# Six transformer layers on one core: the token shift before the feed-forward goes through DMA instead of TensorE, and the transposes of q are evicted bank by bank

## What is computed

```python
def shift_tokens(t):                 # the second half of the channels comes from the token before
    a, s = jnp.split(t, 2, -1)
    s = jnp.pad(s, ((0, 0), (1, 0), (0, 0)))[:, :-1]
    return jnp.concatenate([a, s], -1)
for i in range(6):
    x = attn_layer(shift_tokens(x), Wqkv[i], q_scale[i], k_scale[i], Wo[i]) + x
    x = ffn_layer(shift_tokens(x), ln_g[i], ln_b[i], W1[i], b1[i], W2[i], b2[i]) + x
```

## Time and profile before

| | us |
|---|---|
| median of 3 runs (lowest, highest) | 3981.29 (3973.6, 3982.08) |
| the profiled execution | 3975.59 |
| its span, first to last instruction | 3973.6 |
| TensorE busy | 3731.3 (94%) |
| VectorE busy | 3272.7 (82%) |
| ScalarE busy | 2830.6 (71%) |
| GpSimd busy | 2383.9 (60%) |

### The profile page before, as it was taken

The page is one execution under the profiler, slowest core; times in us unless marked ns, Lnnn a source line. Parts: engine busy times, 40 slices in busy tenths (PEclk is TensorE's granted clock), DMA queues, the critical chain, the costliest instruction groups (busy, mean ns, idle before and its releaser), DMA issues. The chain is left out here.

```text
span 3973.6 us, 160814 instructions
## 1 busy us (share of the span) xinstructions
PE 3731.3 (94%) x70608; PEld 2684.1 (68%) x70608; DVE 3272.7 (82%) x4767; ACT 2830.6 (71%) x4676; POOL 2383.9 (60%) x1968
## 2 busy tenths in 40 slices
PE   5899999967999999999999999999999999999997
PEld 3222222236788878788887888878787888878775
DVE  7899999947888888888888888888888888888884
ACT  2588888856777777777777777777777777777774
POOL 2100000027777777777777777777777777777773
PEclk7799999989999999999999999999999999999998
DMA  2110000014344344344444334434444433443432
GB/s 89 32 52 23 22 18 22 10 32 114 103 106 113 102 111 117 103 105 115 108 108 114 104 100 118 114 100 107 112 109 109 114 103 103 127 109 101 114 107 55
DMA packets 202556, 360.09 MB, mean 91 GB/s; under 512 B 35518, under 2 KB 74050, under 8 KB 201538
## 3 DMA queue, kind: packets, MB, share of 16 engines
q1 hardware_dynamic: 201794, 348.71, 32.7%
HBM read 236.68 MB, written 111.67 MB: 88 GB/s over the span
## 5 line engine op out<-in xcount | busy, mean ns | idle before, releaser
L1120 POOL TENSOR_TENSOR T<-T 128x1024 f32<-128x1024 f32 x384 | 907.3, 2376 | 27.4 <-DVE T L1587 26.6
L1138 POOL TENSOR_TENSOR T<-T,rn 128x1024 f32<-128x1024 f32 x384 | 732.0, 1906 | 27.1 <-POOL rn L1131 0.4
L705 ACT ACTIVATE E<-p_s 128x512 f32<-128x512 f32 x1024 | 555.8, 596 | 167.9 <-PE p_s L565 162.8
L639 DVE TENSOR_REDUCE negmax<-p_max 128x1 f32<-128x1024 f32 x512 | 605.3, 1219 | 50.6 <-PE p_max L545 37.2
L1210 PE MATMUL PA<-Wqkv,XS 128*128 128x512 f32 x2304 | 632.8, 410 | 10.0 <-DVE XS L1548 7.4
L1236 PE MATMUL PD<-ident,T 128*128 128x128 f32 x3072 | 419.6, 280 | 52.5 <-ACT qT L1458 47.3
L1210 PEld LDWEIGHTS PA<-Wqkv,XS 128*128 128x128 f32 x2304 | 414.6, 193 | 79.8 <-DVE XS L1548 10.3
L1595 DVE TENSOR_REDUCE ss<-SQ 128x32 f32<-128x2048 f32 x192 | 436.9, 2275 | 0.0
L1566 DVE TENSOR_REDUCE sm<-Ew 128x16 f32<-128x1024 f32 x192 | 233.7, 1217 | 238.9 <-ACT Ew L1432 238.9
L1236 PEld LDWEIGHTS PD<-ident,T 128*128 128x128 f32 x3072 | 329.7, 141 | 115.7 <-ACT qT L1458 96.4
L1291 PEld LDWEIGHTS PD<-Wo,OT 128*128 128x128 f32 x3072 | 366.3, 192 | 61.2 <-issue 61.2
(11 more groups left out here) (168 smaller groups left out, 6785.0 us busy)
## 6 DMA issues: line engine op xcount, KB each, us to landing
VW<-v_rows SPq DMA_DIRECT2D x768, 256.0 KB, 4.5
v_rows<-Vs SPq DMA_DIRECT2D x192, 512.0 KB, 6.0
Wraw<-in_Wqkv SPq DMA_DIRECT2D x40, 192.0 KB, 5.1
QA<-parts_q SPq DMA_DIRECT2D x384, 16.0 KB
KA<-parts_k SPq DMA_DIRECT2D x192, 32.0 KB
parts_q<-parts SPq DMA_DIRECT2D x8, 384.0 KB, 2.6
parts_k<-parts SPq DMA_DIRECT2D x8, 384.0 KB, 2.7
Wo<-in_Wo SPq DMA_DIRECT2D x12, 256.0 KB, 4.9
```

The source lines that it names most:

```text
L639: dve.tensor_reduce(negmax[:, qh, c, qt:qt + 1], p_max[:, k % 2, :], axis=AX.X, op=ALU.max, negate=True).then_inc(s_mr.sem, 1)
L705: act.activation(E[:, s % 4, c, :], p_s[:, i % 2, :], ACT.Exp, scale=DH ** -0.5)\
L1120: pool.tensor_tensor(out=t_, in0=t_, in1=T2[:, i * HALF:(i + 1) * HALF], op=ALU.add).then_inc(ad.sem, 1)
L1138: pool.tensor_tensor(out=t_, in0=t_, in1=rn[:, p, i * LH:(i + 1) * LH].unsqueeze(2).broadcast_to([P, LH, LD]), op=ALU.mult).then_inc(no.se ...
```

## The change

Four edits, all in `layers`. The shift: the eight transposes a step, their copies on ScalarE and FS are gone; SyncE issues three DMAs instead, in slots d = 3, behind `values_in` and ahead of `values_out`: the second half of the channels of 127 tokens one partition down (from X into fx), row 0 of fx from the small tensor `ends`, and the last token's row into `ends` for the next step. VectorE copies the first half of the channels from X to fx and waits for the DMAs at the start of `ff_stats`. The eight transposes of q signal after each four, and ScalarE copies each four out with an instruction of its own. Those of k wait for the first bank, do four, wait for the second. `FIRST_Q` of the second slot of a step goes from 105 to 130.

```diff
-    te = m.count("l_te", 3)
+    te = m.count("l_te", 4)
+    shd = m.count("l_shift", 48)
...
+        def ff_shift(u):
+
+            xt = X[:, :, u % NT, hc:D]
+            sp.wait_ge(xd.sem, xd.at(B * u + B - 1))
+            if u > 0:
+                sp.wait_ge(f3.sem, f3.at(u - 1))
+                sp.wait_ge(shd.sem, shd.at(u - 1))
+            sp.dma_start(fx[1:P, :, hc:D], xt[0:P - 1]).then_inc(shd.sem, 16)
+            sp.dma_start(fx[0:1, :, hc:D], ends[:, 1 + (u - 1) % 2 if u % NT else 0, :, :]).then_inc(shd.sem, 16)
+            sp.dma_start(ends[:, 1 + u % 2, :, :], xt[P - 1:P]).then_inc(shd.sem, 16)
...
             if is_tile(s - 1):
                 values_in(s - 1)
+            if d == 3 and is_step(u - 1):
+                ff_shift(u - 1)
             if is_tile(s):
                 values_out(s)
...
-    BLOCK, FIRST_Q = 256, (105, 105, 100, 100)
+    BLOCK, FIRST_Q = 256, (105, 130, 100, 100)
...
         def transpose_qk(n, i):
-            free(*fd)
-            pe.wait_ge(no.sem, no.at(n, i + 1))
-            for j in range(PAIRS):
-                lo = i * HALF + j * P
-                mm = pe.transpose(flat(PD)[:, j * P:(j + 1) * P], T1[:, n % 2, lo:lo + P], ident[:, :])
-            mm.then_inc(tq.sem, 1)
-            fd[:] = [(te.sem, te.at(n, 3 if i else 1))] * 2
+            for a in range(2):
+                free(fd[a])
+                if a == 0:
+                    pe.wait_ge(no.sem, no.at(n, i + 1))
+                for j in range(a * 4, a * 4 + 4):
+                    lo = i * HALF + j * P
+                    mm = pe.transpose(flat(PD)[:, j * P:(j + 1) * P], T1[:, n % 2, lo:lo + P], ident[:, :])
+                if i == 0:
+                    mm.then_inc(tq.sem, 1)
+                    fd[a] = (te.sem, te.at(n, a + 1))
+            if i == 1:
+                mm.then_inc(tq.sem, 1)
+                fd[:] = [(te.sem, te.at(n))] * 2
...
         def transpose_q(n):
-            act.wait_ge(tq.sem, tq.at(n, 1))
-            act.activation(qT[:, :, :].rearrange("p j n -> p (j n)"), flat(PD), ACT.Copy).then_inc(te.sem, 1)
+            for a in range(2):
+                act.wait_ge(tq.sem, tq.at(n, a + 1))
+                act.activation(qT[:, a * 4:a * 4 + 4, :].rearrange("p j n -> p (j n)"), PD[:, a, :], ACT.Copy)\
+                    .then_inc(te.sem, 1)
...
         def ff_tokens(u):
-            dve.wait_ge(f2.sem, f2.at(u))
+            dve.wait_ge(xd.sem, xd.at(B * u + B - 1))
             if u > 0:
                 dve.wait_ge(f3.sem, f3.at(u - 1))
-            dve.tensor_copy(fx[:, :, :], PC[:, 1, :].rearrange("p (b n) -> p b n", b=B)).then_inc(f2e.sem, 1)
+            dve.tensor_copy(fx[:, :, 0:hc], X[:, :, u % NT, 0:hc]).then_inc(f2e.sem, 1)

         def ff_stats(u):
             dve.wait_ge(f2e.sem, f2e.at(u))
+            dve.wait_ge(shd.sem, shd.at(u))
```

More of the change, by code:

```diff
@@ L917, in layers @@
     OT = m.sb("OT", [P, PAIRS, P])
-    FS = m.sb("FS", [P, B, P + 1])
+    ends = m.sb("ends", [1, 3, B, hc])
     fx = m.sb("fx", [P, B, D])
@@ L954, in layers @@
     kh = m.count("l_kh")
-    tq = m.count("l_tq", 2)
-    te = m.count("l_te", 3)
+    tq = m.count("l_tq", 3)
+    te = m.count("l_te", 4)
     sc = m.count("l_s")
@@ L1087, in on_pool @@
         pool.memset(kH[:, :, :, :], 0.0).then_inc(s_one.sem, 1)
-        pool.memset(FS[:, :, :], 0.0).then_inc(s_one.sem, 1)
+        pool.memset(ends[:, :, :, :], 0.0).then_inc(s_one.sem, 1)
         lo = LASTW // 32 * 32
@@ L1293, in output @@
             fd[0] = (xd.sem, xd.at(n))
[L1295 to L1310, removed]
         def ff_norm(u):
@@ L1375, in on_pe @@
                 input_T(s + 1)
-            if d == 3 and is_step(u - 1):
-                ff_shift(u - 1)
             if is_tile(s):
                 project_v(s)
-            if d == 3 and is_step(u - 1):
-                ff_tokens(u - 1)
             if d == 1 and is_step(u - 2):
@@ L1465, in transpose_k @@
             act.activation(kH[:, n % B, :, :], src[:, :, P - WIN:P], ACT.Copy).then_inc(te.sem, 1)
[L1467 to L1479, removed]
         def ff_norm(u):
@@ L1510, in on_act @@
                 square(s, 0)
-            if d == 3 and is_step(u - 1):
-                ff_carry(u - 1)
             if d == 2 and is_step(u - 2):
@@ L1648, in on_dve @@
         for j in range(2):
-            dve.tensor_scalar_mul(XS[:, :, j, :], FS[:, :, 0:1].broadcast_to([P, B, P + 2]), 1.0)\
+            dve.tensor_scalar_mul(XS[:, :, j, :], zero[:, :].unsqueeze(2).broadcast_to([P, B, P + 2]), 1.0)\
                 .then_inc(s_one.sem, 1)
```

## The result

| | before | after |
|---|---|---|
| median (lowest to highest), 4 runs each | 3981.68 (3973.6 to 3997.19) | 4476.69 (4468.33 to 4477.44) |
| profiled execution | 3975.59 | 4477.44 |
| its span | 3973.6 | 4475.7 |
| mean granted clock of TensorE | 0.980 | 0.925 |

The ratio is 1.1233, with a 95% interval of 1.1197 to 1.127: the changed kernel is 12% slower.

The account below looks back on a forecast made before the run. TensorE was taken as the bound, or nearly. 3975.6 + 688 (late shift) - 16 (bank by bank) + 7 (FIRST_Q) = 4655 us on the profiled execution, so 4660 for the median; the 8-in-10 range was 4060 to 4900.

Parts of the forecast that it names:

- What bounds: TensorE, busy 61.28 of a 62.75 us step, bounds the kernel; little to win by removing waits, much to lose by one.
- Part 1: Shift by DMA removes eight TensorE transposes and a stall: 1.2 us a step, 58 us over 48 steps if nothing else holds.
- Part 2: Shift DMA queues behind VW, runs 508 pieces on one engine for 11.1 us, and lands at T+17.3 after the attention product.
- The ring: The DMA queue on the one engine the shift needs is free of the VW transfers at about T+5.9.
- The tail: Time from the end of the shift's data to its reported landing: about 0.3 us.
- the price of a piece: Each 256-byte piece of the shift takes 21.9 ns on one engine, so 508 take 11.1 us.
- short pieces go by their bytes: Rival: shift transfer takes 7.4 us, kernel 4485; chance 0.15 together with the Trainium skill's engine rate, which gives 4345.
- the forecast's own case: Shift on one ring at 20 to 29 ns a piece: 4490 to 4845 us, chance 0.57.
- Part 3: VectorE's late statistics delay GpSimd and TensorE, whose clock falls: first slot +14.3 us, +688 over 48 steps.
- Part 4: Copying q's transposes bank by bank starts the attention product 0.11 us sooner in three slots a step: 16 us gained.
- Part 5: FIRST_Q from 105 to 130 lengthens TensorE's stop in the scores of slots d = 1 by 0.14 us: +7 us.
- The lines I had named: Signs expected in the changed profile: VectorE's DMA wait, TensorE's XS wait, low clock, one DMA engine, k's transposes awaiting GpSimd.

Follow-up runs that it names:

- experiment 3: Changed kernel with the shift's three DMAs, still on one DMA engine, issued ahead of values_in instead of behind it: 3931.39 us, ratio 0.986.
- experiments 1 and 2: Changed kernel with the shift's 127 rows split into two DMAs: first 112 + 15 rows, 4223.12 us; second 122 + 5 rows, 4319.68 us.
- experiment 9: Changed kernel with 76 identity transposes on TensorE ahead of the late q projection, result overwritten, to keep it busy: 4433.71 us, ratio 1.1129.
- experiment 11: Changed kernel with shift rows split 112 + 15, issued ahead of values_in, FIRST_Q back at 105, and ScalarE's copy of E in halves: 3873.61 us.
- experiment 8: Changed kernel with the two one-row DMAs issued before the 127-row one: 4473.78 us, ratio 1.1228.

## Why the prediction was right, and which step was off

**What bounds.** Right. TensorE had 1.5 us of rest in a step, so a new wait went into the time nearly whole: 548 us of waiting at VectorE, 495 us of loss.

**Part 1.** Right for its slot: 1.2 a step, lost in the wait; experiment 3 gets 1.25 there once the wait is gone, 0.1 of it by the bank edit. Over the whole kernel the 58 us were too much: with the bank edit's 21 they would make 79, and experiment 3 gains 53. Of the 26 missing 13.5 are the stop in the scores, which grew; the rest is open.

**Part 2, the step that was off.** The issue began at T+2.0 (forecast T+1.95). One engine took all 508 pieces, as the counts of the earlier trace rows said: 18 GB/s after, and experiments 1 and 2 change the landing with the rings alone. The rule of the Trainium skill on 127 partitions (DMA: Bandwidth & Descriptors, "Why a DMA increments its semaphore by 16 and not by 1") agrees with them. The ring was free about when forecast: the last short piece moved at 2335.40, and 7.2 us back from there is T+5.65, against T+5.9. The tail was longer: VectorE went on 0.76 after that piece, not 0.3. The term that was mis-sized is the price of a piece: I took 21.9 ns, halfway between a 512-byte piece and a 4-byte one, and it is 14.1. The transfer took 7.2 us, not 11.1, and VectorE started at T+13.86 in the mean, not T+17.3. So the price alone makes 3.9 x 48 = 187 us too much, start and tail give some 22 back, and 165 of the 183 us are left to the landing.

The rival "short pieces go by their bytes" had it (7.4 us, 4485) and got a chance of 0.15. So the sign and the place were earned, but that the result fell into the range of 4060 to 4900 is owed to the rival for whose sake it was made wide; the forecast's own case missed it. (Its bounds don't fit its price either: at 20 ns a piece the sum is 4615; 4490 needs some 15 ns.) Against the rival stood only the 4-byte pieces; but at 14.5 ns they are as dear as a 256-byte one is here. Read as a floor for every piece, and with the bytes at 17.5 KB/us (14.6 ns for 256), they give the larger of the two: 14.6. To take the middle was to add part of a floor to a price that was already above it.

The same rival named the Trainium skill's figure for one engine (the same page, Specifications), some 27 GiB/s, by which the transfer would take an estimated 4.5 us and the kernel 4345. The runs speak against it for these pieces: 18 GB/s. That there is no penalty for short pieces within SBUF, as the Trainium skill also states there ("Why small descriptors are slow (HBM only)"), agrees as far as the rows go: the 256-byte piece costs 14.1 ns, half of the 29.3 of the 512-byte one of the earlier trace rows, which went to DRAM.

**Part 3.** Right. From VectorE's start to the next T 14.0 were forecast, 12.7 for the chain and 1.3 for the clock. The mean is 13.79 (13.40 in the step shown), and 12.75 with the clock kept (experiment 9): the chain came out within 0.1, and the clock costs 1.0, between my ends of 0 and 2.5. Which engine is last depends on the clock: in the step shown its loss made TensorE the last (k was normalised at 2345.73 and its transposes started at 2346.23, right behind E), and with the clock kept GpSimd is the last by 0.80.

**Part 4.** 16 forecast, 21 measured alone. The next in line was the copy of E, as said; experiment 11 removes it.

**Part 5.** +7 forecast; +5.0 in the trace, nothing in the time that can be told from zero.

**The sum again**, with what was measured: 4660 - 165 (landing, 3.44 x 48) - 10 (chain and clock, 0.21 x 48) - 5 (bank) - 2 (jump) = 4478, against 4476.69. That it closes to 1 us is partly chance; a profiled execution stands some us off the median. By the step shown alone it doesn't close: its landing and chain are shorter than the mean, and some 30 us would be missing. One step read closely gives the mechanism, the mean of all gives the sum.

**The lines I had named.** VectorE's wait of 10 to 16 (11.4), the clock at 0.50 once a step, one DMA engine at work: all there, though the last ends at T+12.9 and not at T+17. TensorE's wait for XS was to be over 10 and is 9.50 in the step shown, 10.07 in the next; k's wait for GpSimd is the rule only with the clock kept.

## What to carry to other kernels

A DMA's price has two halves: how long it runs, and what is already in the queue where it is issued. Here one transfer of 7.2 us cost 12% behind 1 MB of other loads and nothing when issued 10 us earlier, at a point where its data were ready too; so look for the earliest safe place in the queue's list before making it faster. Count the completion writes of DMAs of other shapes in the trace to see on how many engines yours will run, and choose the rows of a piecewise transfer (112 + 15, not 127) by that. After a wait is removed, name what stands next: splitting one copy gave 21 us, splitting the next 40 more.

## What the runs showed that was not expected

- The issue right behind the 508-piece DMA holds SyncE itself. How long SyncE stood in that issue in the changed kernel (lowest, median, highest, ns):

```profile
L1059 SPq DMA_DIRECT2D fx<-ends x48: 6521/8658/9140, 1003.7 to 4439.9; - x48
```

  With two rings it is 5.0 us, with the rows spread 0.6 to 0.95 an issue, and in experiment 8 it moves to v_rows. Whatever stands behind it in SyncE's list is late by that. The 0.4 an issue that I counted for the three was too low even without the stand: 0.72 and 0.57 for the other two.
- DMAs within SBUF aren't cheap to issue, short or long: medians of 0.68 us for the one of 112 rows, 0.94 for 15 rows and 0.60 to 0.66 for 1 row (experiment 1), against 0.43 for one of the four of VW. So it isn't the number of engines; what it is wasn't tried.
- A piece of 256 bytes within SBUF takes 14.1 ns on one engine, a 4-byte one 14.5.
- After a stop of TensorE of 4.2 us the projections behind it already ran at the lower clock in part (experiment 1, 2.02 + 2.76); with one of 9.5 us the clock was low for 10.2 us.
